# Fewer weight columns for the products of three offsets in a convolution and channel-mix kernel

## The chip, the cores and the metric

The kernel runs on one core of a Trainium2 chip. The metric is the device time of one execution in microseconds (us). A core has five engines that run their own instruction streams: TensorE (PE; its weight loads are listed apart as PEld), VectorE (DVE), ScalarE (ACT), GpSimd (POOL) and SyncE (SP), which here only issues DMAs. They wait for each other through semaphores. TensorE keeps one operand, the weights, in its array and streams the other, up to 512 columns, past it; sums are formed in PSUM.

## The reference

```python
# x: (64, 128, 2048); cond: (64, 128); conv weight: (128, 32, 9), 4 groups; mix weight: (8, 128, 128, 1)
y = x + conv1d(x, weight, padding=4, groups=4) + (cond @ c_weight.T)[:, :, None] + bias[None, :, None]
h = gelu(cond @ W0 + b0); h = gelu(h @ W1 + b1); att = softmax(h @ W2 + b2)       # (64, 8)
agg_w = einsum('bk,koi->boi', att, mix_w[..., 0]); agg_b = att @ bias_k
out = y + einsum('boi,bih->boh', agg_w, y) + agg_b[:, :, None]
```

Each of the 64 samples gets a grouped convolution of 9 taps over 2048 positions (32 input and 32 output channels in each of four groups), with its input added back, and then a 128 by 128 matrix of its own, again with the input added back. Everything is float32.

## The kernel before

The 2048 positions of a sample are cut into 4 phases (position modulo 4) of 512. One product on TensorE takes the 32 input channels of one group as rows, 512 positions of one phase as the moving columns, and weights of 32 rows by 128 columns. The 128 columns are 4 output phases (r = 0 to 3) times 32 output channels, so one product feeds all four output phases of the group. Twelve such offsets m = 0 to 11 (`M = K + PH - 1`) cover 9 taps at 4 output phases: offset m serves output phase r when 0 <= m - r < 9. For m = 0 only the first 32 of the 128 columns of weights are other than zero, for m = 1 the first 64, for m = 2 the first 96; for m = 9, 10 and 11 the zeros stand at the front.

For accuracy x and the weights are split in a high and a low part of the type fp32r: x_hi with cw_hi, x_hi with cw_lo, and x_lo with cw_hi. So the convolution of a sample takes 3 x 12 = 36 products for each group (`CONV`), and the mixing takes 3 x 4 = 12 products for each of the four output phases (`MIX`), 32 rows by 128 columns too: 48 steps of four products.

`conv_step(s, g, i)` makes product i of group g (line 429): for i below 24 it goes through `OUTER + INNER`, twice for each offset (cw_hi, then cw_lo), with x_hi; for the last 12 through `INNER + OUTER` with x_lo. `mix_step` makes the mixing products (line 460). The four groups take different rows of the array and write four different banks of PSUM. `slot(s)` issues the four groups in turn at every step; group t runs `LAG * t` = 0, 2, 4 or 6 steps behind. A slot is the convolution of sample s followed by the mixing of sample s - 2. The first product of a group (`start`) overwrites its bank, the last (`stop`) releases ScalarE through `y_ready`.

Around it, for each sample: ScalarE turns the loaded x into phases (L508), VectorE splits it in x_hi (L595) and x_lo (L601); ScalarE rounds the result to y_hi (L521) and VectorE forms y_lo (L612); GpSimd builds the sample's matrix (L739 to L757), which goes to DRAM and comes back four times as mix_rep, under the four row groups; ScalarE moves the mixed result out (L534) and SP stores it. The orders are written out by hand for each engine by `pipeline`.

Of the kernel before, what the change touches and what calls it, by code (L numbers as in the profile page):

```python
# [11 lines left out]
P = 128  # L12
PH = 4
U = 4
Q = 32
# [1 line left out]
AHEAD = 4  # L17
LAG = 2
MIX_LATE = 2
OUTER, INNER = (0, 8, 1, 9, 2, 10, 3, 11), (4, 5, 6, 7)  # L20


def after(sample, lag):
# [9 lines left out]
def done(sample, each=1, lag=0):  # L33

    n, k = sample
    return n * (U * each) + (k + 1 + lag) * each


def buf(sample):
    return sample[1] % 2  # L40
# [14 lines left out]
def cond_resid_kernel(nc, x, cond, bias, conv_w, ctx_w, w0, b0, w1, b1, w2, b2, mix_w, mix_b, out):  # L55
# [15 lines left out]
    with ExitStack() as stack:  # L71
# [29 lines left out]
        def x_at(tile, rows, m):  # L101

            return tile[rows, m % PH, m // PH:m // PH + H, :]
# [112 lines left out]
        def exists(sample):  # L216
            n, _ = sample
            return not isinstance(n, int) or 0 <= n < ROUNDS

        def is_sample(s, b):  # L220
            return isinstance(s[0], int) and number(s) == b
# [12 lines left out]
        def y_at(s):  # L234
            return z_ps if is_sample(s, 1) else y_ps
# [97 lines left out]
        def _(pe):  # L333
# [10 lines left out]
            for k in range(K):  # L344
                for g in range(G):
                    rows = slice(Q * g, Q * g + Q)
                    mm = pe.matmul(wt_ps[rows, k, :], cw_nat[rows, :, k], ident[rows, rows],
                                   start=True, stop=k != K // 2)
                if k == K // 2:
                    for g in range(G):  # L350
                        rows = slice(Q * g, Q * g + Q)
                        mm = pe.matmul(wt_ps[rows, k, :], ident[rows, rows], ident[rows, rows],
                                       start=False, stop=True)
# [46 lines left out]
            def conv_step(s, g, i):  # L400

                if not exists(s):
                    return
                rows = slice(Q * g, Q * g + Q)
                if i == 0:
                    if g == 0:
                        if is_sample(s, 0):
                            pe.wait_ge(x_first_phase, 1)
                        else:
                            pe.wait_ge(x_hi_made, done(s))  # L410
                    if is_sample(s, 1):
                        if g == 0:
                            pe.wait_ge(table_made, 2)
                    elif is_sample(s, 2):
                        pe.wait_ge(y_lo_made, g + 1)
                    elif not is_sample(s, 0):

                        pe.wait_ge(y_lo_made, done(s, G, lag=-2) + g + 1)
                if g == 0 and i in (4, 8) and is_sample(s, 0):
                    pe.wait_ge(x_first_phase, i // 4 + 1)  # L420
                if g == 0 and i == 12 and is_sample(s, 0):
                    pe.wait_ge(x_hi_made, 1)
                if g == 0 and i == 2 * M:
                    pe.wait_ge(x_lo_made, done(s))
                if i < 2 * M:
                    m, w, xx = (OUTER + INNER)[i // 2], (cw_hi, cw_lo)[i % 2], x_hi
                else:
                    m, w, xx = (INNER + OUTER)[i - 2 * M], cw_hi, x_lo
                mm = pe.matmul(y_at(s)[:, g, :], w[rows, m, :], x_at(xx[buf(s)], rows, m),  # L429
                               start=i == 0, stop=i == CONV - 1)  # L430
                if i == CONV - 1:
                    mm.then_inc(y_ready, 1)
# [39 lines left out]
            def step(s, t, i):  # L472
                if steps(s) == MIX:
                    mix_step(after(s, -MIX_LATE), t, i)
                elif i < CONV:
                    conv_step(s, t, i)
                else:
                    mix_step(after(s, -MIX_LATE), t, i - CONV)
# [312 lines left out]
```

## Time and profile before

| | us |
|---|---|
| median of 3 runs | 726.35 |
| lowest, highest | 726.35, 726.84 |
| the profiled execution | 728.89 |
| its span, first to last instruction | 726.9 |
| PE busy | 716.2 (99%) |
| PEld busy | 701.7 (97%) |
| ACT busy | 601.3 (83%) |
| POOL busy | 546.9 (75%) |
| DVE busy | 462.2 (64%) |

Busy time is the time in which an engine has at least one instruction running; products on TensorE overlap, so its share does not say how much of the array's peak is used. Waiting of an engine counts only where the engine is the one that the end waits for. The start of a product to the start of the next one of the same group of rows is the measure that the text below uses.

### The profile page before, as it was taken

How to read it: one execution, taken by the hardware profiler on the slowest of the kernel's cores; microseconds unless marked ns; L12 is line 12 of the kernel's file. 1: busy time of each engine (PE TensorE's matmuls, PEld its weight loads, DVE VectorE, ACT ScalarE, POOL GpSimd, SP SyncE). 2: the span in 40 equal slices, each digit the busy share in tenths (PEclk: the TensorE clock that was granted, in tenths of full speed). 3: DMA queues.
4: the chain of work that ended last, by engine and by line, in shares of the span. 5: the costliest groups of instructions: out<-in, count | busy, mean ns of one | idle time of the engine just before them, and what ended most of it. 6: DMA issues, size and time to landing. Idle time of an engine off the chain costs nothing.

```text
span 726.9 us, 29222 instructions
## 1 busy us (share of the span) xinstructions
PE 716.2 (99%) x12417; PEld 701.7 (97%) x12417; DVE 462.2 (64%) x411; ACT 601.3 (83%) x458; POOL 546.9 (75%) x592
## 2 busy tenths in 40 slices
PE   8999999999999999999999999999999999999996
PEld 6799999999999999999999999999999999999996
DVE  4897676576776675575575575575575575575543
ACT  5988888878888888888988888888888988888843
POOL 2799999999999999967767767767767767767750
PEclk9999999999999999999999999999999999999999
DMA  6345858768777877877787778777777767767546
GB/s 208 140 152 200 274 202 281 244 213 298 251 250 261 274 253 248 285 244 246 268 280 260 251 272 294 244 238 275 245 242 275 245 238 275 245 243 271 191 151 243
DMA packets 66551, 177.56 MB, mean 244 GB/s; under 512 B 7437, under 2 KB 50008, under 8 KB 50264
## 3 DMA queue, kind: packets, MB, share of 16 engines
q1 hardware_dynamic: 66002, 176.93, 71.5%
q8 instruction: 25, 0.41, 0.2%
q10 hardware_dynamic: 518, 0.17, 0.1%
q14 instruction: 6, 0.05, 0.0%
HBM read 101.57 MB, written 75.50 MB: 244 GB/s over the span
## 4 chain that ended last, share of the span: by engine, by line
PE 81%; POOL 11%; DMA 5%; SPq 1%; issue 1%; DVE 0%; ACT 0%; DVEq 0%; POOLq 0%; ACTq 0%
PE ps L429 60%; PE ps L460 21%; POOL mix_prod L744 4%; POOL mix_prod L739 4%; DMA mix_dram<-mix_parts 3%; POOL mix_sum_f L747 1%; DMA x_in<-in_x_dram 1%; SPq L290 1%; POOL mix_f L751 1%; DMA mix_rep<-mix_dram 1%; POOL mix_parts L757 1%; POOL mix_parts L754 0%; POOL par L734 0%; POOL par L763 0%; ACT x_hi L512 0%
## 5 line engine op out<-in xcount | busy, mean ns | idle before, releaser
L429 PE MATMUL ps<-x_hi,cw_hi 32*128 32x512 f32 x3072 | 406.0, 387 | 0.8 <-ACT x_hi L512 0.5
L429 PE MATMUL ps<-x_hi,cw_lo 32*128 32x512 f32 x3072 | 405.0, 386 | 0.0
L508 ACT ACTIVATE x_ph<-x_in 128x2560 f32<-128x2560 f32 x63 | 318.7, 5060 | 2.7 <-DMA x_in<-in_x_dram 2.2
L612 DVE TENSOR_TENSOR y_lo<-ps,y_hi 128x512 fp32r<-128x512 f32 x256 | 159.1, 683 | 241.1 <-ACT y_hi L521 241.1
L429 PE MATMUL ps<-x_lo,cw_hi 32*128 32x512 f32 x3072 | 275.6, 385 | 0.0
L429 PEld LDWEIGHTS ps<-x_lo,cw_hi 32*128 32x128 f32 x3072 | 240.0, 183 | 2.3 <-issue 0.8
L429 PEld LDWEIGHTS ps<-x_hi,cw_hi 32*128 32x128 f32 x3072 | 219.5, 184 | 3.8 <-issue 1.6
L429 PEld LDWEIGHTS ps<-x_hi,cw_lo 32*128 32x128 f32 x3072 | 219.1, 184 | 1.6 <-issue 0.2
L460 PE MATMUL ps<-y_hi,mix_rep 32*128 32x512 f32 x2048 | 215.1, 384 | 2.1 <-DMA mix_rep<-mix_dram 2.1
L534 ACT ACTIVATE z_out<-ps,par 128x1024 f32<-128x1024 f32 x124 | 146.5, 1242 | 74.5 <-PE ps L460 74.5
L601 DVE TENSOR_TENSOR x_lo<-x_ph,x_hi 128x2560 fp32r<-128x2560 f32 x63 | 190.0, 3016 | 2.1
L460 PEld LDWEIGHTS ps<-y_hi,mix_rep 32*128 32x128 f32 x2048 | 182.3, 183 | 4.3 <-issue 1.8
L744 POOL TENSOR_TENSOR mix_prod<-mix_prod 128x512 f32<-128x512 f32 (+1 forms) x128 | 165.3, 1291 | 10.0
L521 ACT ACTIVATE y_hi<-ps 128x512 fp32r<-128x512 f32 x256 | 132.9, 603 | 32.1 <-PE ps L429 32.0
L460 PE MATMUL ps<-y_lo,mix_rep 32*128 32x512 f32 x1024 | 158.1, 384 | 0.0
L739 POOL TENSOR_TENSOR mix_prod<-mixw_t,par 128x512 f32<-128x512 f32 x128 | 147.2, 1171 | 5.2
L734 POOL COPY par<-table 128x9 f32 (+1 forms) x63 | 68.9, 1094 | 108.0 <-ACT z_out L534 102.2
L460 PEld LDWEIGHTS ps<-y_lo,mix_rep 32*128 32x128 f32 x1024 | 125.2, 183 | 0.6
L595 DVE CAST x_hi<-x_ph 128x2560 fp32r<-128x2560 f32 x63 | 100.9, 1601 | 0.3 <-ACT x_ph L508 0.3
L747 POOL TENSOR_TENSOR mix_sum_f<-mix_prod 128x128 f32<-128x128 f32 x64 | 45.4, 710 | 5.0
L751 POOL TENSOR_TENSOR mix_f<-mix_sum_f,ident 128x128 f32<-128x128 f32 x64 | 40.8, 637 | 5.0
L754 POOL TENSOR_TENSOR mix_parts<-mix_sum_f,ident 128x128 fp32r<-128x128 f32 x64 | 39.9, 623 | 0.0
(79 smaller groups left out, 94.9 us busy)
## 6 DMA issues: line engine op xcount, KB each, us to landing
x_in<-in_x_dram SPq DMA_DIRECT2D x64, 1024.0 KB, 7.0
out_dram<-z_out SPq DMA_DIRECT2D x63, 1024.0 KB, 5.0
mix_rep<-mix_dram SPq DMA_DIRECT2D x256, 128.0 KB, 2.7
mix_dram<-mix_parts SPq DMA_DIRECT2D x64, 128.0 KB, 5.7
out_dram<-x_in SPq DMA_DIRECT2D x2, 512.0 KB, 4.0
z_out<-in_L_cond_weight_dram SPq DMA_DIRECT2D x1, 512.0 KB, 4.0
cw_nat<-in_L_cond_weight_dram SPq DMA_DIRECT2D x1, 144.0 KB, 2.2
w_sb<-in_L_cond_W_dram ACTq DMA_DIRECT2D x2, 64.0 KB, 5.0
```

Of the source, the lines that this page charges most:

```text
L429: mm = pe.matmul(y_at(s)[:, g, :], w[rows, m, :], x_at(xx[buf(s)], rows, m), start=i == 0, stop=i == CONV - 1)
L460: mm = pe.matmul(z_at(s)[:, r, :], rep_at(s)[rows, g, h, :], yy[s[1]][rows, g, :], start=i == 0, stop=i == MIX - 1)
L508: nc.scalar.activation(x_ph[buf(s)][:, :, :, :], by_lane(x_in[buf(s)]), ACT.Copy).then_inc(x_split_ph, 1)
L521: nc.scalar.activation(y_hi[s[1]][:, g, :], y_at(s)[:, g, :], ACT.Copy).then_inc(y_hi_made, 1)
L534: nc.scalar.activation(out_lanes(z_out[buf(s)], pair), z_lanes(z_at(s), pair), ACT.Identity, bias=par[s[1]][:, NK:NK + 1]).then_inc(z_read, 1)
L595: nc.vector.tensor_copy(x_hi[buf(s)][:, :, :, :], x_ph[buf(s)][:, :, :, :]).then_inc(x_hi_made, 1)
L601: nc.vector.tensor_tensor(x_lo[buf(s)][:, :, :, :], x_ph[buf(s)][:, :, :, :], x_hi[buf(s)][:, :, :, :].bitcast(F32), ALU.subtract).then_in ...
L612: nc.vector.tensor_tensor(y_lo[s[1]][:, g, :], y_at(s)[:, g, :], y_hi[s[1]][:, g, :].bitcast(F32), ALU.subtract).then_inc(y_lo_made, 1)
L734: nc.gpsimd.tensor_copy(par[s[1]][:, :], table[:, number(s), :]).then_inc(par_made, 1)
L739: nc.gpsimd.tensor_tensor(mix_prod[:, ks, :], mixw_t[:, ks, :], par[s[1]][:, ks].unsqueeze(2).broadcast_to([P, NK // 2, P]), ALU.mult).the ...
L744: nc.gpsimd.tensor_tensor(mix_prod[:, 0:half, :], mix_prod[:, 0:half, :], mix_prod[:, half:2 * half, :], ALU.add).then_inc(mix_sum, 1)
L747: nc.gpsimd.tensor_tensor(mix_sum_f[:, :], mix_prod[:, 0, :], mix_prod[:, 1, :], ALU.add).then_inc(mix_sum, 1)
```

## The change

The order of the outer offsets begins with offset 8 in place of offset 0, so that the first product of every group, which overwrites its bank, still has all 128 columns. The products of offset m take only the first `max(80, 32 * (m + 1))` columns of weights and write that many partitions of the bank: 80 for m = 0 and 1, 96 for m = 2, 128 for all others. The columns left out are zeros.

```diff
-OUTER, INNER = (0, 8, 1, 9, 2, 10, 3, 11), (4, 5, 6, 7)
+OUTER, INNER = (8, 0, 9, 1, 10, 2, 11, 3), (4, 5, 6, 7)
+NARROW = 80
...
-                mm = pe.matmul(y_at(s)[:, g, :], w[rows, m, :], x_at(xx[buf(s)], rows, m),
+                wide = min(P, max(NARROW, Q * (m + 1)))
+                mm = pe.matmul(y_at(s)[0:wide, g, :], w[rows, m, 0:wide], x_at(xx[buf(s)], rows, m),
                                start=i == 0, stop=i == CONV - 1)
```

Offsets 8 and 0 read the same phase of x (m modulo 4), as do 9 and 1, 10 and 2, 11 and 3, so the first four products of a group still need phase 0 alone, the next four phase 1, and so on.

On TensorE, at the start of the first sample's convolution, the products stood in this order before (a row is the size of the output, partitions by columns; the groups join one after the other, so runs of one kind grow to four):

```order
L429 MATMUL ps<-x_hi,cw_hi 128x512
L429 MATMUL ps<-x_hi,cw_lo 128x512
L429 MATMUL ps<-x_hi,cw_hi 128x512 x2
L429 MATMUL ps<-x_hi,cw_lo 128x512 x2
L429 MATMUL ps<-x_hi,cw_hi 128x512 x3
L429 MATMUL ps<-x_hi,cw_lo 128x512 x3
```

and now, at the same place:

```order
L431 MATMUL ps<-x_hi,cw_hi 128x512
L431 MATMUL ps<-x_hi,cw_lo 128x512
L431 MATMUL ps<-x_hi,cw_hi 80x512
L431 MATMUL ps<-x_hi,cw_hi 128x512
L431 MATMUL ps<-x_hi,cw_lo 80x512
L431 MATMUL ps<-x_hi,cw_lo 128x512
L431 MATMUL ps<-x_hi,cw_hi 128x512
L431 MATMUL ps<-x_hi,cw_hi 80x512
L431 MATMUL ps<-x_hi,cw_hi 128x512
```

The number of products is the same; the first group's third and fourth product (offset 0) have 80 columns, while the group beside it is at offset 8 with 128. Since the groups are two steps apart, narrow and full products of different groups alternate in the stream.

In the part of the last sample where the four groups go over to x_lo (also on TensorE) the rows were these before:

```order
L429 MATMUL ps<-x_lo,cw_hi 128x512 x3
L429 MATMUL ps<-x_hi,cw_hi 128x512
L429 MATMUL ps<-x_lo,cw_hi 128x512 x3
L429 MATMUL ps<-x_hi,cw_lo 128x512
L429 MATMUL ps<-x_lo,cw_hi 128x512 x24
```

and are these now:

```order
L431 MATMUL ps<-x_lo,cw_hi 128x512 x3
L431 MATMUL ps<-x_hi,cw_hi 128x512
L431 MATMUL ps<-x_lo,cw_hi 80x512
L431 MATMUL ps<-x_lo,cw_hi 128x512 x2
L431 MATMUL ps<-x_hi,cw_lo 128x512
L431 MATMUL ps<-x_lo,cw_hi 128x512 x4
L431 MATMUL ps<-x_lo,cw_hi 80x512 x2
L431 MATMUL ps<-x_lo,cw_hi 128x512 x6
L431 MATMUL ps<-x_lo,cw_hi 96x512
```

Here each narrow product is a single step of its group, between full ones. On the other engines and in their waits nothing moves.

## Rows read from the trace of the kernel before

**Rows 1.** The page, busy time, share of the span and count by engine.
```profile
PE 716.2 (99%) x12417; PEld 701.7 (97%) x12417; DVE 462.2 (64%) x411; ACT 601.3 (83%) x458; POOL 546.9 (75%) x592
```

**Rows 2.** Two stretches: length, busy time (instructions) by engine, clock, DMA share, GB/s.
```profile
100.00:149.00 49.00, 47.95 (x840) 47.06 (x844) 31.16 (x29) 39.69 (x32) 45.19 (x45) 1.00 0.74 251
149.00:700.00 551.00, 551.00 (x9728) 547.78 (x9724) 349.26 (x302) 470.06 (x352) 420.59 (x463) 1.00 0.75 254
```

**Rows 3.** Waits: who waited for whom, us in total, times, longest.
```profile
PE ps L460 <- DMA mix_rep<-mix_dram: 2.1, 2, 1.1
```

**Rows 4.** The chain that ended last, longest pieces: start, us, what.
```profile
109.76 7.21 DMA mix_dram<-mix_parts
120.30 8.02 DMA mix_dram<-mix_parts
...
149.24 6.83 PE ps L429 x122
171.18 6.82 PE ps L429 x121
182.06 6.82 PE ps L429 x121
...
704.30 6.82 PE ps L429 x121
712.46 8.17 PE ps L460 x133
```

**Rows 5.** The page, groups: count, busy us, mean ns of one, idle before.
```profile
L429 PE MATMUL ps<-x_hi,cw_hi 32*128 32x512 f32 x3072 | 406.0, 387 | 0.8 <-ACT x_hi L512 0.5
L429 PEld LDWEIGHTS ps<-x_lo,cw_hi 32*128 32x128 f32 x3072 | 240.0, 183 | 2.3 <-issue 0.8
```

**Rows 6.** Timeline of PE, then of PEld, all four groups running: start, us, engine, what.
```profile
301.56 0.43 PE L429 MATMUL ps<-x_hi,cw_hi 32*128 32x512 f32 x4
301.78 0.43 PE L429 MATMUL ps<-x_hi,cw_lo 32*128 32x512 f32 x4
...
301.56 0.23 PEld L429 LDWEIGHTS ps<-x_hi,cw_lo 32*128 32x128 f32 x4
301.79 0.23 PEld L429 LDWEIGHTS ps<-x_hi,cw_hi 32*128 32x128 f32 x4
```

**Rows 7.** Timeline of the last products, where one group runs alone.
```profile
719.78 0.84 PE L460 MATMUL ps<-y_lo,mix_rep 32*128 32x512 f32 x4
...
720.01 0.18 PEld L460 LDWEIGHTS ps<-y_lo,mix_rep 32*128 32x128 f32 x1
```

**Rows 8.** Timeline of PEld after a pause, windows ending at 25.45 and 25.70.
```profile
25.39 0.19 PEld L429 LDWEIGHTS ps<-x_lo,cw_hi 32*128 32x128 f32 x4
...
25.39 0.30 PEld L429 LDWEIGHTS ps<-x_lo,cw_hi 32*128 32x128 f32 x8
```

**Rows 9.** Weight loads of two widths, groups by shape: count, busy us, mean ns.
```profile
L364 PEld LDWEIGHTS ps<-h,w_sb 128*128 128x128 f32 x2 | 0.3, 188 | 0.4 <-ACT h L562 0.4
L377 PEld LDWEIGHTS ps<-w_sb,h 128*64 128x64 f32 x2 | 0.2, 134 | 0.4 <-ACT h L564 0.4
```

**Rows 10.** Timeline of PE near the start, one group's next products.
```profile
12.17 0.62 PE L429 MATMUL ps<-x_hi,cw_hi 32*128 32x512 f32 x1
...
12.60 0.62 PE L429 MATMUL ps<-x_hi,cw_lo 32*128 32x512 f32 x1
```

**Rows 11.** Timeline of PE where 32-row products give way to a 64-row one.
```profile
20.71 0.39 PE L429 MATMUL ps<-x_hi,cw_lo 32*128 32x512 f32 x1
...
21.04 1.12 PE L384 MATMUL ps<-z_out,ones 64*128 64x512 f32 x2
```

## The prediction, made before the changed kernel had run

> **What bounds the kernel now.** I read the busy times first, then the stretches, the waits and the chain, and last the timeline of TensorE. TensorE has work for 99% of the span, its weight loads for 97% [rows 1]. From 149 to 700 us it is never without a product (551.00 of 551.00 us), while ACT is busy for 470 us and POOL for 421 [rows 2]. Before 149 us it misses 1.05 us of 49, with POOL busy for 92% of the time, and the chain goes through the matrix on its way to DRAM [rows 2, 4]; TensorE's waits for mix_rep are 2.1 us in all [rows 3]. From 149 us on the chain is TensorE alone. Its slot repeats every 10.88 us (171.18 to 182.06), and 10.88 / 48 steps is 0.2267 us for four products, one of each group [rows 4]. The timeline shows the same: rounds of four start at 301.56 and 301.78 [rows 6]. So the kernel's time is 0.2267 us times the steps, and the change must be judged by what it does to this pitch.
>
> What sets 0.2267 us? Near the start a group's next product comes 0.43 us later (12.17 to 12.60), 512 columns at 1.2 GHz being 0.4267 [rows 10]; at twice that rate, 2.4 GHz, the columns alone would take 0.2133. The pitch is 0.0133 us above this floor. Two readings fit the number. In the one, four weight loads go one after another through one port, 56.7 ns each (a quarter of 0.2267), and it is the loads that bind. In the other each group has 13.3 ns of its own between streams, whatever its weights are. Two places tell them apart. At the end of the program one group runs alone: the row at 719.78 holds one product of another group and three of this one, and 0.84 - 0.38 = 0.46 us for two distances gives 0.23 [rows 7]. That is the pitch with four groups, though only this group's weights were loaded. And after a pause four loads are seen in 0.19 us and eight in 0.30, so the second four start 0.11 us after the first four, which themselves start within 0.01 us: groups load side by side, and a load of 128 columns is out of the way after 0.11 us, half of the pitch [rows 8]. In the steady state the load for the next step starts with the stream of this one (both 301.56) and its record ends after 0.18, 0.04 before the next product [rows 5, 6]. So the load is hidden, and I take the second reading.
>
> **The change part by part.** The three narrow offsets take 3 x 3 = 9 of 48 steps of a group in a sample, 9 x 64 = 576 in the program. Nothing is added or removed on any engine.
>
> The shorter load: 64 columns fewer take 188 - 134 = 54 ns off a load's record, 0.84 ns a column [rows 9]. So 80 columns should read 183 - 40 = 143 ns, and 96 columns 183 - 27 = 156. The load lies under a stream of at least 0.2133 us and ended 0.04 us before it was needed even at full width. Value: nothing. What hides it is the stream of the product before. The stream itself keeps its 512 columns.
>
> The page "TensorE: Matmul & The Clock Gate", section "LDWEIGHTS (loading the stationary operand)", of the Trainium skill says that a load's time follows its columns and not its rows; the difference of 54 ns for 64 columns has its slope of 1/1.2 ns a column. The same page's section "Back-to-back issue gap" gives an isolated product N/2.4 + 2.5 ns, 215.8 for 512 columns; the trace does not agree, 226.7. By that floor the most that the narrow steps could return would be 10.9 ns each, 6.3 us, which is inside the range below.
>
> The bounds, since no row shows a narrow load under such a stream. If the 13.3 ns were owed to the load, a narrow step could fall to 0.2133: 576 x 13.3 ns = 7.7 us less. From the other side, products of different width shift the groups against each other, and the trace shows that the pitch depends on how they lie: the two slots from 149.24 to 171.18, soon after a wait, take 10.97 us each, the later ones 10.88 [rows 4]. A loss of 0.09 us over 62 slots is 5.6 us. I take zero, the value of the group that ran alone.
>
> The order: offset 8 ahead of 0 changes no wait, as the pair reads the same phase. The first product of a group, which needs y_lo and x_hi, is as wide as before. Value: nothing. Writing 80 or 96 partitions of a bank in place of 128: the bank is read only after the last product, whose offset (11 or 3) has all columns, so nobody waits for less. Nothing.
>
> The sum: span 726.9, change 0, and 2.0 us around the span make the profiled execution's 728.9. The median of the runs is 2.5 us lower, 726.35; I forecast 726.3. A difference below 0.2% (1.5 us) is what a measurement of this kernel could not tell from none.
>
> **The rivals.**
>
> The gap between streams goes with the load. If the weights' last step, after the stream, takes its time from the number of columns, 13.3 ns x 48/128 = 5 ns go for 80 columns and 3.3 for 96: 6 x 5 + 3 x 3.3 = 40 ns a sample, 2.6 us, and 723.8 us. If a narrow load takes the whole gap away, a sample gains 9 x 13.3 = 120 ns. Up to 149 us the chain through POOL and mix_dram keeps that, and (712 - 149) / 10.88 = 52 samples give 6.2 us: 720.1. For both: the loads are busy for 97% of the time and their record ends only 0.04 us before the next product. Against: the place where 128 columns were out of the way after 0.11 us, and near the start, at half the rate, where no gap is seen though loads were as wide.
>
> One port for all loads. A load of 128 columns would then take 56.7 ns, 53.3 for its columns and 3.3 beside them, so the 48 steps' loads come to 4 x (39 x 136 + 6 x 88 + 3 x 104) = 24,576 cycles of 2.4 GHz, which is just 48 x 512. If the slack of narrow steps carried over, every step would fall to 0.2133: 48 x 13.3 = 0.64 us a slot over 52 slots, 33 us, 693 us. ACT's 470 of 551 us would still fit. That the numbers meet speaks for it; against it the single group at 0.23 and the four loads at once, which I hold to be strong.
>
> Slower: the groups lose their spacing. Where a narrow product lets its group start some ns early, its stream meets that of another group at the distance that cost 10.97 us a slot. It decides as soon as one slot's end leaves the groups as they lay before 171 us and the next cannot restore them. Twelve edges between widths in each group of each slot speak for it; against it, that the program went from 10.97 to 10.88 by itself and stayed there for 50 slots. Price: 0.09 x 62 = 5.6 us, 732 us.
>
> Slower by much: a width is a mode. Going from 32 to 64 rows the next product started 0.33 us after the round before (20.71 to 21.04), 0.10 over the pitch [rows 11]. At 12 edges for each group and slot this would be 12 x 0.10 x 64 = 77 us if the groups switch apart, 803 us. The page "TensorEngine Tiling (Array Packing)", section "Key Properties", of the Trainium skill says that changing the tiling mode drains TensorE, and its table has columns of 32, 64 and 128 only; by it 80 and 96 columns stay in the mode of 128, which is why I give this little.
>
> **How the numbers follow.** No change, 726.3: 0.42. Part of the gap goes, 723.8: 0.16. All of it in the narrow steps, 720.1: 0.17. One port, 693: 0.06. Lost spacing, 732: 0.16. A mode, 803: 0.03. Faster by over 0.2% is 0.39, within 0.2% 0.42, slower 0.19. The range is 718 to 732: it ends below at the whole gap with no loss before 149 us (726.3 - 7.7 = 718.6), above at the lost spacing, and leaves out the port and the mode, about 0.09, and some of what lies at its ends. The likeliest case's own range is 725.5 to 727.
>
> **What would show it.** Narrow loads at 143 and 156 ns show that the change does what it says. The pitch decides the rest: rounds of narrow products 0.2267 us after the round before and slots of 10.88 us prove the forecast; 10.76 is the whole gap, 10.84 a part, 10.24 the port (then with waits of TensorE for mix_rep or x_hi), 10.97 the lost spacing. I am wrong if the slot differs from 10.88 by more than 0.02 us while TensorE is still never without work.

## The result: slower by half a per cent

The changed kernel took 732.77 us (median of 8 runs, 731.56 to 734.23); the kernel before 728.55 us (8 runs, the three that were shown among them, 726.35 to 731.74). The ratio is 1.0053, with a 95% interval of 1.003 to 1.0077. The forecast was 726.3 us, with 718 to 732 as its range: the time lies outside it and on the side that had 0.19. The kernel before itself came out 2.2 us above the median of those three, which the ratio takes out: 726.35 x 1.0053 would be 730.2 us. So of the distance between forecast and time the change made about 4 us and the level of the kernel before the other 2.2; without these the time would lie inside the range, and the forecast of no change would be wrong all the same, by 0.53%. Ratios here and below leave out slow executions; there was one, of the run with the order alone, with 899.59 us at a granted clock of 0.75.

The page's first line of the changed kernel, which answers to [rows 1]:

```profile
PE 720.0 (99%) x12417; PEld 662.9 (91%) x12417; DVE 462.4 (63%) x411; ACT 600.9 (82%) x458; POOL 540.1 (74%) x592
```

The weight loads are busy for 39 us less, and that bought nothing: the span went from 726.9 to 730.1 us. The groups of weight loads by shape say that the edit does what it was to do (count, busy us, mean ns; full loads stay at 183):

```profile
L431 PEld LDWEIGHTS ps<-x_hi,cw_lo 32*80 32x80 f32 x512 | 59.6, 144 | 2.5
L431 PEld LDWEIGHTS ps<-x_hi,cw_lo 32*96 32x96 f32 x256 | 40.1, 156 | 0.3
```

The chain of the changed kernel, longest pieces (start, us, what), beside [rows 4]:

```profile
147.85 7.33 PE ps L431 x126
158.82 7.33 PE ps L431 x125
...
696.18 7.33 PE ps L431 x125
```

Only the distances of the starts count, as the pieces are cut at other products. From 147.85 to 696.18 us there are 50 slots of 10.967 us. In the kernel before 50 slots from 149.24 on take 2 x 10.97 + 48 x 10.88 = 544.2 us; here they take 548.3. These 4.1 us hold the whole difference of 3.2 us between the spans; the rest of the program gives back 0.9.

TensorE was never without a product in these slots, as before (length, busy us by engine, clock):

```profile
149.00:700.00 551.00, 551.00 (x9654) 508.81 (x9651) 346.42 (x301) 468.45 (x351) 409.69 (x460) 1.00 0.74 252
```

In the timeline the rounds lie as follows, the changed kernel first, then the kernel before at the corresponding place:

```profile
312.17 0.41 PE L431 MATMUL ps<-x_hi,cw_lo 32*128 32x512 f32 x2
...
312.40 0.43 PE L431 MATMUL ps<-x_hi,cw_hi 32*80 32x512 f32 x4
312.63 0.43 PE L431 MATMUL ps<-x_hi,cw_lo 32*80 32x512 f32 x4
312.86 0.44 PE L431 MATMUL ps<-x_hi,cw_hi 32*128 32x512 f32 x4
```

```profile
312.21 0.39 PE L429 MATMUL ps<-x_hi,cw_lo 32*128 32x512 f32 x2
...
312.44 0.43 PE L429 MATMUL ps<-x_hi,cw_hi 32*128 32x512 f32 x4
312.66 0.43 PE L429 MATMUL ps<-x_hi,cw_lo 32*128 32x512 f32 x4
312.89 0.43 PE L429 MATMUL ps<-x_hi,cw_hi 32*128 32x512 f32 x4
```

A row of four is named after its first product (the groups are two steps apart, so a "32*80 x4" holds full ones too). From the first to the last start shown are 0.69 us with narrow products in them and 0.68 without; over a slot it adds up to 0.087 us, though each narrow load is shorter by 27 to 39 ns. The starts in the trace, averaged over the slots from 200 to 700 us, say where it lies: a round in a stretch of full products takes 0.2267 us, the rounds around narrow ones mostly 0.228 to 0.237.

### The profile page after: what moved, and what is told of

Its sections match the earlier page's. It is cut to its first block, busy times and chain, and to the rows that moved or that the text cites. A ratio compares the mean times of both kernels' runs of the same rounds, so it can differ in the third digit from the quotient of the medians.

```text
span 730.1 us, 29222 instructions
## 1 busy us (share of the span) xinstructions
PE 720.0 (99%) x12417; PEld 662.9 (91%) x12417; DVE 462.4 (63%) x411; ACT 600.9 (82%) x458; POOL 540.1 (74%) x592
## 4 chain that ended last, share of the span: by engine, by line
PE 80%; POOL 11%; DMA 5%; SPq 1%; issue 1%; DVE 0%; ACT 0%; DVEq 0%; POOLq 0%; ACTq 0%
PE ps L431 59%; PE ps L462 20%; POOL mix_prod L746 5%; DMA mix_dram<-mix_parts 4%; POOL mix_prod L741 4%; POOL mix_sum_f L749 1%; SPq L291 1%; DMA mix_rep<-mix_dram 1%; POOL mix_f L753 1%; POOL mix_parts L759 1%; POOL mix_parts L756 0%; SPq L306 0%; PE ps L338 0%; POOL par L736 0%; POOL par L765 0%
## 5 line engine op out<-in xcount | busy, mean ns | idle before, releaser
L431 PE MATMUL ps<-x_hi,cw_hi 32*128 32x512 f32 (+2 forms) x3072 | 404.2, 389 | 1.2 <-ACT x_hi L514 1.0
L431 PE MATMUL ps<-x_hi,cw_lo 32*128 32x512 f32 (+2 forms) x3072 | 402.6, 387 | 0.0
L431 PE MATMUL ps<-x_lo,cw_hi 32*128 32x512 f32 (+2 forms) x3072 | 276.6, 387 | 0.0
L431 PEld LDWEIGHTS ps<-x_lo,cw_hi 32*128 32x128 f32 (+2 forms) x3072 | 231.9, 174 | 11.5 <-issue 0.8
L431 PEld LDWEIGHTS ps<-x_hi,cw_hi 32*128 32x128 f32 (+2 forms) x3072 | 215.7, 175 | 14.8 <-issue 1.9
L431 PEld LDWEIGHTS ps<-x_hi,cw_lo 32*128 32x128 f32 (+2 forms) x3072 | 215.8, 174 | 11.3 <-issue 0.2
L462 PEld LDWEIGHTS ps<-y_hi,mix_rep 32*128 32x128 f32 x2048 | 178.2, 183 | 13.2 <-issue 2.7
L746 POOL TENSOR_TENSOR mix_prod<-mix_prod 128x512 f32<-128x512 f32 (+1 forms) x128 | 162.6, 1271 | 10.0
L736 POOL COPY par<-table 128x9 f32 (+1 forms) x63 | 76.0, 1206 | 119.1 <-ACT z_out L536 114.2
L759 POOL TENSOR_TENSOR mix_parts<-mix_f,mix_parts 128x128 fp32r<-128x128 f32 x64 | 34.5, 539 | 5.0
```

The lines of the kernel that those rows point to most:

```text
L431: mm = pe.matmul(y_at(s)[0:wide, g, :], w[rows, m, 0:wide], x_at(xx[buf(s)], rows, m), start=i == 0, stop=i == CONV - 1)
L462: mm = pe.matmul(z_at(s)[:, r, :], rep_at(s)[rows, g, h, :], yy[s[1]][rows, g, :], start=i == 0, stop=i == MIX - 1)
L736: nc.gpsimd.tensor_copy(par[s[1]][:, :], table[:, number(s), :]).then_inc(par_made, 1)
L746: nc.gpsimd.tensor_tensor(mix_prod[:, 0:half, :], mix_prod[:, 0:half, :], mix_prod[:, half:2 * half, :], ALU.add).then_inc(mix_sum, 1)
```

## The experiments

Five kernels below are probes: they are the kernel before with products appended after its own work, each stretch on a line of its own, so that the row of a stretch gives its pitch. The last start of x10 products is the row's length less the last record, 0.38 to 0.40 us, after the first, so the pitch is about (length - 0.38) / 9. For slow stretches this comes out up to 2 ns too long; where the text gives four digits they are from the starts in the trace. The code of a probe is shown for one stretch, in short. The others change the kernel itself and are compared by slot and ratio.

### First probe: stretches of one width

```diff
+for n in range(32):
+    for g in range(4):            # or one group
+        wide = P if n in (0, 31) else 80      # or 128, 96, 64, alternating
+        pe.matmul(y_ps[0:wide, g, :], cw_hi[Q * g:Q * g + Q, 5, 0:wide], y_hi[0][Q * g:Q * g + Q, 0, :], start=n == 0, stop=n == 31)
```

> The kernel before, with products of one shape appended after its own work: 32 steps each with one group of rows or with four, and weights of 128, 80, alternately 128 and 80, and 96 columns (four groups also 64). Only the pitch inside each stretch counts. If narrow weights cost by themselves (theory A: about 9 ns for each product of 80 columns, as in the changed kernel's timeline), one group at 80 columns goes at 0.236 us and alternating at 0.231, against 0.227 at 128. If a change of width costs (B), one group at 80 stays at 0.227 and alternating rises. If only the meeting of groups costs (C), one group stays at 0.227 in all stretches, and four groups rise where their widths differ (alternating in opposite phase most). If the gap over 0.213 belonged to the load, 80 would fall to 0.222 or 0.213.

Timeline of the first products (always full ones) of four stretches with four groups each: all 80 columns (L526), alternately 128 and 80 (L530), the same with groups 1 and 3 wide where 0 and 2 are narrow (L534), and 96 columns (L538):

```profile
784.12 0.41 PE L526 MATMUL ps<-y_hi,cw_hi 32*128 32x512 f32 x3
...
791.58 0.39 PE L530 MATMUL ps<-y_hi,cw_hi 32*128 32x512 f32 x3
...
799.04 0.39 PE L534 MATMUL ps<-y_hi,cw_hi 32*128 32x512 f32 x2
...
806.30 0.57 PE L538 MATMUL ps<-y_hi,cw_hi 32*128 32x512 f32 x3
```

By these starts the first two stretches take 7.46 / 32 = 0.233 us a step, where the kernel before has 0.2267 (10.88 / 48) and so has the last stretch of this probe, with all products full. So the loss is there without any of the kernel's waits, and a stretch in which half of the products are narrow is as slow as one in which all are. The third stretch does not fit that: two of its groups took 7.26 / 32 = 0.2268 us a step, no loss at all though every second product was narrow, and the other two 0.233. None of the theories here explains it. 96 and 64 columns had 0.230. The one-group stretches did not answer, since the array's clock fell to its lower level (more under the last heading).

### The order alone

```diff
-OUTER, INNER = (0, 8, 1, 9, 2, 10, 3, 11), (4, 5, 6, 7)
+OUTER, INNER = (8, 0, 9, 1, 10, 2, 11, 3), (4, 5, 6, 7)
```

> The new order of the offsets with all products at 128 columns. All theories: as before, ratio 1.000 within 0.002, slots of 10.88 us. If the order has a part in the loss, it is over 1.002.

Ratio 0.9997 (0.9979 to 1.0015), slots of 10.88 us. The order has no part in it.

### Narrow products side by side

```diff
-                    m, w, xx = (OUTER + INNER)[i // 2], (cw_hi, cw_lo)[i % 2], x_hi
+                    order = OUTER + INNER if is_sample(s, 0) else (8, 9, 10, 11, 0, 1, 2, 3, 4, 5, 6, 7)
+                    m, w, xx = order[i // 2], (cw_hi, cw_lo)[i % 2], x_hi
...
-                    m, w, xx = (INNER + OUTER)[i - 2 * M], cw_hi, x_lo
+                    m, w, xx = (4, 5, 6, 7, 8, 9, 10, 11, 0, 1, 2, 3)[i - 2 * M], cw_hi, x_lo
```

> The widths of the change, but each group takes its offsets 0, 1 and 2 one after the other (first sample apart), so that a group has 4 changes of width in a slot in place of 12, with the same 9 narrow products. If a narrow product costs by itself (A), the slot stays at 10.96 to 10.97 us and the ratio at 1.005. If changes of width cost (B), a third of the loss is left: 10.91 us, ratio 1.002. If the groups' meeting costs (C), between the two.

Ratio 1.002 (1.0004 to 1.0036), slots of 10.94 us (292.69, 303.63 and 314.57 in its chain): two thirds of the loss stay. Neither cost by the product alone (10.97) nor by the change of width alone (10.91, or 10.92 with the steps from 80 to 96 columns counted too, which makes 6 changes of 12) fits.

### Nearly all products narrow

```diff
-                wide = min(P, max(NARROW, Q * (m + 1)))
+                wide = P if i in (0, CONV - 1) else NARROW
```

> All products of the convolution at 80 columns except the first and the last of a group (leaves out output phases 2 and 3 of most offsets). 34 of 48 products of a group are narrow, with 2 changes back and forth. Cost by the product (A): 34 x 9 ns = 0.31 us a slot, 11.19 us, ratio 1.027. By changes of width or the mix of widths (B, C): at or below 10.90 us, ratio 1.00. If the gap belonged to the load: 10.4 to 10.7 us, ratio 0.97 to 0.98.

Ratio 1.0187 (1.0161 to 1.0214), slots of 11.13 us. The loss of 0.25 us for 34 products is 7.4 ns each. It grows with the narrow products while the changes of width go down from 12 to 2, so it is not the changes that cost; by the product it is somewhat less than supposed.

### Second probe: one group alone at full rate

```diff
+for n in range(11):
+    for g in (0,):
+        wide = P if n in (0, 10) else 80      # or 128, 96, alternating
+        pe.matmul(y_ps[0:wide, g, 0:512], cw_hi[rows_of(g), 5, 0:wide], y_hi[0][rows_of(g), 0, 0:512], start=n == 0, stop=n == 10)
```

> As the first probe, but stretches with one group are kept to 11 products, since there the pitch of one group fell to 0.427 us (512 columns at 1.2 GHz) after some 13 products at 0.227, and two stretches of four groups are preceded by short products of 136, 272 and 408 columns in groups 1, 2 and 3, which pull the groups 57 ns apart. Cost by the product (A): one group at 80 columns at 0.233 to 0.236 us. Meeting of groups (C): one group at 0.227 at every width, two and three groups at 80 above it, four at 80 at 0.233 when close together and 0.227 when 57 ns apart. If the gap over 0.213 belonged to the load: one group at 80 at 0.222 or less. With 384 columns the pitch of one group is 0.173 us if the gap of 13.3 ns is a constant, 0.170 if it is a share of the stream.

The first nine products of three stretches with one group, at 128, 80 and 96 columns; here the pitch is (length - 0.38) / 8:

```profile
734.59 2.20 PE L517 MATMUL ps<-y_hi,cw_hi 32*128 32x512 f32 x9
...
741.62 2.25 PE L525 MATMUL ps<-y_hi,cw_hi 32*128 32x512 f32 x9
...
755.84 2.23 PE L541 MATMUL ps<-y_hi,cw_hi 32*128 32x512 f32 x9
```

That gives 0.2275, 0.234 and 0.231 us; by the starts it is 0.2266, 0.233 and 0.230. A single group with nobody beside it is slower with narrow weights: the meeting of groups, which my rival had, is not needed. With streams of 384 columns the two widths hardly differ (rows of 1.74 us for 128 and 1.71 for 80 columns). Stretches with the groups pulled apart did not keep their spacing (at 80 columns three groups went together and one some 0.1 us away from them) and tell nothing.

### The groups pulled apart in the changed kernel

```diff
-            with eng.Fori(2, last) as n:
+            with eng.Fori(2, 4) as n:
+                for k in range(U):
+                    slot((n, k))
+            for s in range(U * 4, U * 5):
+                slot((s // U, s % U))
+            with eng.Fori(5, last) as n:
...
+                if i == 0 and g > 0 and is_sample(s, 16):
+                    pe.matmul(y_at(s)[:, g, 0:136 * g], cw_hi[rows, 8, :], x_hi[0][rows, 0, 0:H, :].rearrange("p h l -> p (h l)")[:, 0:136 * g], start=True, stop=True)
```

> The changed kernel with one more short product of 136, 272 and 408 columns in groups 1, 2 and 3 ahead of sample 16, once (its fifth round is written out beside the loop for that). Meeting of groups (C): from sample 16 on the slot is 10.88 us in place of 10.97, and the ratio to the kernel before falls from 1.005 to about 1.000. Cost by the product (A): 10.97 us and 1.005 stay.

Ratio 1.0119 (1.0087 to 1.0152); its slots are 10.97 us from 283.76 us on. That agrees with a cost by the product, but is no test of the spacing: up to 274 us its chain still went through mix_dram, TensorE waited nine times for mix_rep (4.4 us), and after these waits the four groups lay within some 0.05 us of each other in a round, as they do in the changed kernel. Why the waits lasted longer I have not looked into.

### Third probe: ten widths

> The kernel before with stretches of 12 products of one group appended, each behind 12 steps of four groups at 128 columns, over widths of 128, 120, 112, 104, 96, 88, 80, 72, 64 and 32 columns, 80 columns taken from the far end of the tile, and streams of 448, 480 and 256 columns at 128 and at 80. Cost by the product (A): the pitch of a group alone depends on the width, 0.2267 us at 128, 0.230 at 96, 0.233 at 80 as in the second probe, and no width lies below 0.2267 (else a version with that width would beat the kernel before). If the load were what sets the pitch, it would fall with the width. Streams of 384 columns had 0.173 at both widths, so the cost should be gone at 256 and perhaps at 448.

Timeline, one group, 12 products each (the row holds ten): 128, 120, 112, 104, 96, 88, 80 and 64 columns from the start of the offset's row, and last 80 columns from column 48:

```profile
730.21 2.42 PE L513 MATMUL ps<-y_hi,cw_hi 32*128 32x512 f32 x10
...
735.66 2.49 PE L521 MATMUL ps<-y_hi,cw_hi 32*120 32x512 f32 x10
...
741.21 2.45 PE L529 MATMUL ps<-y_hi,cw_hi 32*112 32x512 f32 x10
...
746.68 2.44 PE L537 MATMUL ps<-y_hi,cw_hi 32*104 32x512 f32 x10
...
752.20 2.46 PE L545 MATMUL ps<-y_hi,cw_hi 32*96 32x512 f32 x10
...
757.70 2.42 PE L553 MATMUL ps<-y_hi,cw_hi 32*88 32x512 f32 x10
...
763.13 2.50 PE L561 MATMUL ps<-y_hi,cw_hi 32*80 32x512 f32 x10
...
775.76 2.45 PE L577 MATMUL ps<-y_hi,cw_hi 32*64 32x512 f32 x10
...
786.78 2.42 PE L593 MATMUL ps<-y_hi,cw_hi 32*80 32x512 f32 x10
```

2.42 us is a pitch of 0.2267, 2.49 and 2.50 of 0.234. There is no trend with the width: 88 columns cost nothing, 120 as much as 80, and 80 columns read from another place nothing at all. This is where the theory of a cost by the product fell. With shorter streams the two widths lie within 1 ns of each other (448 columns: 0.2028 us at 128, 0.2036 at 80; 480 columns: 0.2162 and 0.2172). But at these lengths the full products themselves stand 16 ns above what the columns take at 2.4 GHz, not 13.3, so the gap is no constant for full weights either.

### No two narrow products in a row

```diff
-                    m, w, xx = (OUTER + INNER)[i // 2], (cw_hi, cw_lo)[i % 2], x_hi
+                    m, w, xx = (OUTER + INNER)[i // 4 * 2 + i % 2], (cw_hi, cw_lo)[i // 2 % 2], x_hi
```

> The widths of the change with each pair of offsets taken as hi, hi, lo, lo in place of hi, lo, hi, lo (8 hi, 0 hi, 8 lo, 0 lo), so that no two narrow products of a group follow each other: 18 changes of width in a slot in place of 12, 9 narrow products as before. If the cost goes by the product alone, the slot stays at 10.97 us and the ratio at 1.005. If a narrow product between full ones costs 13.3 ns and one in a run 6.7 (the first probe's 0.2332 us for both all 80 and alternating), the slot is 10.88 + 6 x 13.3 + 3 x 6.7 = 10.98 us, and 1.006.

Ratio 1.0068 (1.0035 to 1.0101), slots of 10.97 us (300.60, 311.57). The two expectations, 10.97 and 10.98, lie too close for the run to choose.

### 96 columns for all three offsets

```diff
-NARROW = 80
+NARROW = 96
```

> The changed kernel with 96 columns for all three offsets in place of 80, 80 and 96. Cost by the product, half as large at 96 (3.3 ns against 6.7, the probes' 0.230 against 0.233): the loss of 0.087 us a slot falls to about 0.05, slot 10.93 us, ratio 1.003. If any change of width costs the same, 10.97 and 1.005 stay.

Ratio 1.0101 (1.0078 to 1.0124), slots of 11.00 us (294.65, 305.65): more loss with fewer columns left out. Both expectations missed. The loss in the kernel is not the sum of the probes' means; why, no run shows.

### Fourth probe: widths and places

> The third probe's widths again in another order, 80 columns twice and from columns 16, 32 and 48 of the tile, 88 from 0 and 40, 120 from 0 and 8, 96 from 0 and 32, and stretches that alternate 128 with 88, 120 and 80. Theory D (each width has its own pitch against a fixed cadence of the engine, set by the width alone): 80 at 0.2334 us from every place and both times, 88 at 0.2266, 120 at 0.2336. Theory E (the place in SBUF from which the weights are read decides): 80 from column 48 again at 0.2266, from 0 at 0.2334. Theory F (chance, how the stretch happens to begin): the same width comes out both ways.

80 columns from 0, 16, 32 and 48 and again from 0; 120 from 0 and from 8; 96 from 0 and from 32:

```profile
730.08 2.50 PE L513 MATMUL ps<-y_hi,cw_hi 32*80 32x512 f32 x10
...
735.83 2.46 PE L521 MATMUL ps<-y_hi,cw_hi 32*80 32x512 f32 x10
...
741.33 2.44 PE L529 MATMUL ps<-y_hi,cw_hi 32*80 32x512 f32 x10
...
747.02 2.42 PE L537 MATMUL ps<-y_hi,cw_hi 32*80 32x512 f32 x10
...
752.46 2.50 PE L545 MATMUL ps<-y_hi,cw_hi 32*80 32x512 f32 x10
...
769.32 2.49 PE L569 MATMUL ps<-y_hi,cw_hi 32*120 32x512 f32 x10
...
774.88 2.42 PE L577 MATMUL ps<-y_hi,cw_hi 32*120 32x512 f32 x10
...
780.55 2.46 PE L585 MATMUL ps<-y_hi,cw_hi 32*96 32x512 f32 x10
...
786.04 2.42 PE L593 MATMUL ps<-y_hi,cw_hi 32*96 32x512 f32 x10
```

The same width comes out the same when it is repeated behind the same kind of lead-in, so it is not chance; and it changes with the place, so it is not the width. Everything that ends at column 128 takes 0.2267 us, whatever its width, and the 80 columns that end at 96 take what the 96 that end there take. Of the stretches that alternate, 128 with 88 has 0.2267 us, 128 with 120 0.2303 and 128 with 80 0.2319.

### Widths without a cost: 88

```diff
-                wide = min(P, max(NARROW, Q * (m + 1)))
+                wide = 88 if m < 2 else P
```

> The changed kernel with 88 columns for offsets 0 and 1 and 128 for offset 2, so that only widths are used whose pitch alone was 0.2266 us in the third probe. If the pitch of each width decides (D): slots of 10.88 us, ratio 1.000. If it is the change of width in a group's stream that costs, whatever the widths: about 10.95 us, ratio 1.004 to 1.006.

Ratio 1.0005 (0.9987 to 1.0024), slots of 10.88 us (300.71, 311.59). Narrow products and changes of width in a group's stream cost nothing if the read ends at 88.

### 8 columns fewer, with a cost: 120

```diff
-NARROW = 80
+NARROW = 120
```

> The changed kernel with 120 columns for the three offsets: 8 columns fewer than before. If the loss grew with the columns left out, nothing would be left of it (8 of 48 columns: 10.89 us, ratio 1.001). If the irregular pitch of widths decides (D; 120 alone took 0.2336 us): slot 10.94 to 11.0 us, ratio 1.005 to 1.010.

Ratio 1.0042 (1.0024 to 1.006), slots of 10.96 us (304.42, 315.38). Leaving out 8 columns costs almost what the change costs.

### Fifth probe: full width from other places

> Stretches of 12 products of one group as in the third and fourth probe: 128 columns of weights taken from columns 0 to 120 past the start of an offset's row, 128 columns with the stream taken 4 to 64 elements later, and 80 columns from 0, 8 and 48 and with a shifted stream. Theory E, made sharper by the fourth probe (the column at which the read of the weights ends decides: 80, 96, 112 and 120 have pitches of 0.2334, 0.230, 0.229 and 0.2336 us, while 88 and 128 have 0.2267, wherever the read begins): 128 columns from 8 end like 8 (as yet unseen), from 80 like 80, so some of the full-width stretches must lie above 0.2267 us. Theory D (width alone): all stretches with 128 columns stay at 0.2267. If some stretch lies below 0.2267, a version of the kernel before with its weights at that place would beat both.

128 columns that begin 0, 4, 8 and 64 columns past the start of the row; then 128 columns from the start with the stream taken 8 elements later; then 80 columns from column 8:

```profile
728.12 2.42 PE L516 MATMUL ps<-y_hi,cw_hi 32*128 32x512 f32 x10
...
746.18 2.42 PE L540 MATMUL ps<-y_hi,cw_hi 32*128 32x512 f32 x10
...
751.63 2.48 PE L548 MATMUL ps<-y_hi,cw_hi 32*128 32x512 f32 x10
...
793.48 2.42 PE L604 MATMUL ps<-y_hi,cw_hi 32*128 32x512 f32 x10
...
826.53 2.49 PE L652 MATMUL ps<-y_hi,cw_hi 32*128 32x512 f32 x10
...
862.80 2.42 PE L700 MATMUL ps<-y_hi,cw_hi 32*80 32x512 f32 x10
```

Full products lose as much as narrow ones when they are read from a place that does not suit, and so they do when the stream is moved by 8 elements against them. 80 columns from column 8 end at 88, like the 88 from 0, and are as fast. Of 16 places for full weights only 0, 4 and 64 had 0.2267 us, and none was below it: there is nothing here with which to beat the kernel before. With the stream taken 64 elements later the first four distances were 0.226 to 0.233 us and the next ones 0.2267.

### The change's own widths, read from the far end

```diff
-                mm = pe.matmul(y_at(s)[0:wide, g, :], w[rows, m, 0:wide], x_at(xx[buf(s)], rows, m),
+                mm = pe.matmul(y_at(s)[0:wide, g, :], w[rows, m, P - wide:P], x_at(xx[buf(s)], rows, m),
```

> The changed kernel with the same widths of 80, 80 and 96 in the same order, the weights taken from the last columns of the offset's row in place of the first (for offsets 0, 1 and 2 these are other weights, so it leaves out their share of the convolution). Theory E: the reads end at column 128 as the full ones do, 0.2266 us each, so slots of 10.88 us and a ratio of 1.000. Theory D, or any cost of the width or of its change: 10.97 us and 1.005.

Ratio 0.9997 (0.9979 to 1.0014). Its chain:

```profile
290.35 6.81 PE ps L431 x121
301.23 6.81 PE ps L431 x121
312.11 6.81 PE ps L431 x121
```

Slots of 10.88 us with the same widths, order and instructions. What differs from the changed kernel is the address from which narrow weights are read, and with it their values (more of them are zeros), and the loss is gone. That it is not the values the fourth probe shows: there 80 columns of offset 5, which has no block of zeros, took 0.2337 us from column 0 and 0.2267 from 48.

## Why the prediction was wrong

- **What bounds the kernel** was right: TensorE's pitch, 0.2267 us a step. The weight load is hidden; the loads read 144 and 156 ns, as forecast (143, 156), and gave no time back. One port for all loads, a width as a mode, and a gap that shrinks with the load are all refuted: 88 columns and the far-end kernel stand at 10.88 us.
- **The step that failed** is "each group has 13.3 ns of its own between streams, whatever its weights are", and with it the value of nothing for the narrow loads, where the runs show a loss of 0.087 us a slot. In the stretches of one group with 512 columns the gap is 13.3 ns only where the read of the weights and the stream lie well to each other in SBUF. With reads that end at column 80 the mean gap is 20 ns, at 96 about 17. All products of the kernel before happen to lie well: by the shapes of its tiles full weights end a multiple of 128 columns from each other, and streams begin a multiple of 64 elements apart. So its trace had a single number for the gap and I took it for a constant. The bounds of an operation that the trace did not show were sought in its duration only, not in where it reads.
- **The rival "the groups lose their spacing"** had the right slot, 10.97 us, and nearly the right time, 732 us, by coincidence: it priced the loss at 5.6 us where 4.2 were measured, and the 2.2 us by which the kernel before came out higher did the rest. One group alone loses too, and the mechanism is another. Its price was also misread: the two slots of 10.97 us in [rows 4] are not a matter of spacing. In the kernel before the first mixing product at 155.87 us has a record of 0.45 us and the next follows 0.29 us later,

```profile
155.87 0.45 PE L460 MATMUL ps<-y_hi,mix_rep 32*128 32x512 f32 x1
...
156.16 0.38 PE L460 MATMUL ps<-y_hi,mix_rep 32*128 32x512 f32 x1
```

  a pause of some 0.06 us, too short for the view of waits; the next slot has the same at 166.84 us. The weight load of that product, which reads mix_rep, begins only 0.05 us before it, where in the slot after these two it begins 0.22 us before its product (177.57 to 177.79; in brackets, how long PEld had been idle):

```profile
155.82 0.18 PEld L460 LDWEIGHTS ps<-y_hi,mix_rep 32*128 32x128 f32 x1 [0.17 <-issue]
...
177.57 0.18 PEld L460 LDWEIGHTS ps<-y_hi,mix_rep 32*128 32x128 f32 x1
```

  The last copy of mix_rep lands at 155.70 and 166.68 us, just ahead of these two loads, and at 176.82 in the next slot, long before. So it is that wait, and a few rounds of 0.233 to 0.236 us behind each pause make up the rest of the 0.09 us.
- **The order, the partial banks and the other engines** were rightly put at nothing: 0.9997 for the order alone, and 0.9997 for the far-end kernel, which writes the same parts of the banks.
- **The size.** Nine narrow products in 48 steps cost a group 87 ns a slot, 9.7 ns each. The probes' means for 80 columns are 6.7 ns a product in a run and 10.5 (one group) to 13.3 (four groups) where every second product is narrow; both orders occur here, so the size fits between them, but the loss at 96 and 120 columns (0.12 and 0.08 us a slot) was not worked out from the probes.

What stays open is the rule. Reads of different widths with the same end within the first 128 columns came out alike, within 1 ns (ends at 88, 96, 112 and 128), and ends at 88, 128, 132 and 192 are good. But a full read that ends at 152, 64 columns past 88, took 0.2336 us, and 64 columns that end at 64, 128 short of 192, took 0.230, so it is a period of neither 64 nor 128 columns. The place is not all of it either: in the first probe two groups lost nothing with reads that end at 80 (L534), and one group of full products at a good place, begun behind two longer distances (0.32 and 0.34 us), needed nine of 0.224 to 0.236 us before it went at 0.2267. So how the products lie in time has a part that was not tested. Whether the cause is a conflict between the two reads in SBUF or something in how the weights enter the array, these runs do not tell.

## What to carry to other kernels

A weight load that is hidden can still raise the pitch of the products by where it reads. Before narrowing or shifting an operand on a saturated TensorE, measure the pitch of a dozen such products by themselves; keep the ends of weight reads and the starts of streams where the full-width products have them. And if a single number stands for a quantity in the trace, ask whether the kernel has ever varied what it may depend on.

## What the runs showed of the hardware

- The pitch of products with 32 rows and 512 columns of fp32r at the full clock depended on the end of the weight read and the start of the stream: 0.2267 us at best, up to 0.2338, at widths from 32 to 128 (one group, first nine distances, third to fifth probe).
- A single group of 32 rows did not hold TensorE's clock in the first probe. Behind 16 products on all 128 rows, its products followed at 0.224 to 0.236 us, then at 0.227, and from 731.0 us on at 0.427, and the granted clock of the stretch from 735 to 749 us reads 0.50, the lower level (length, busy us by engine, clock):

```profile
735.00:749.00 14.00, 14.00 (x35) 8.28 (x34) 0.00 (x0) 0.00 (x0) 0.00 (x0) 0.50 0.00 0
```

  TensorE had been without a pause since 725.7 us. At that level no width differed from another: 0.4267 us for 128, 80 and 96 columns.
- With streams of 256 columns the 80 columns from the start of the row were faster than 128, in one stretch of 12 products each: 0.113 against 0.120 us once they had settled (the first three distances at 80 columns were 0.118). At that length the narrow load did pay.
